# Laying out the node stages of a four-layer graph network in another order, with more turns between a tile's stages

## The reference

```python
h = relu(layernorm(x)); x = x + gcn(h)      # scatter-add over edges, W, norms, LN, relu, + h
h = relu(layernorm(x)); x = x + attn(h)     # 8-head edge attention, skip, LN, GELU FFN (512), LN
h = relu(layernorm(x)); x = x + gat(h)      # GAT with 3 heads, elu, GAT with 1 head
h = relu(layernorm(x)); x = x + sage(h)     # two SAGE layers with batch norm
```

## Time and profile before

| | us |
|---|---|
| median of 3 runs (3016.8 to 3020.15) | 3018.6 |
| the profiled execution | 3018.48 |
| its span | 3016.8 |
| node stage gcn, from its first products to the first gather of the edge pass | 571 to 657.3 |
| node stage attn, from den(0) to the first gather | 1215.8 to 1351.4 |
| node stage gat1, likewise | 1925.8 to 2047.9 |

### The profile page before, as it was taken

One profiled execution on the slowest core, in us unless ns is written; L12 is line 12 of the kernel. 1 busy time (PEld: TensorE's weight loads), 2 busy tenths in 40 slices (PEclk: granted clock), 3 DMA queues, 4 the chain that ended last, 5 costly groups with the idle time before them and its releaser, 6 DMA issues.

```text
span 3016.8 us, 36316 instructions
## 1 busy us (share of the span) xinstructions
PE 2401.5 (80%) x12365; PEld 1783.0 (59%) x12365; DVE 1385.6 (46%) x2998; ACT 927.1 (31%) x1992; POOL 1374.9 (46%) x1431
## 2 busy tenths in 40 slices
PE   6799999748888986667888786685777777499998
PEld 5566666527776775455555554355777766266666
DVE  6756655447677775434454544232222222611313
ACT  4423222223333332543444443231222222300201
POOL 3200000177777773447777773327777775300000
PEclk7577778879889897767999998685555555699999
DMA  9578854049899994106777776204555554465360
GB/s 207 154 238 298 289 198 163 1 138 277 252 264 272 258 269 122 30 20 184 248 243 238 242 236 196 74 19 102 137 129 136 130 136 106 145 202 166 118 202 27
DMA packets 518578, 517.76 MB, mean 172 GB/s; under 512 B 154113, under 2 KB 463748, under 8 KB 517212
## 3 DMA queue, kind: packets, MB, share of 16 engines
q1 hardware_dynamic: 310333, 267.24, 29.6%
q0 software_dynamic: 50528, 115.22, 15.1%
q10 hardware_dynamic: 157534, 132.98, 14.3%
HBM read 301.13 MB, written 227.33 MB: 175 GB/s over the span
## 4 chain that ended last, share of the span: by engine, by line
PE 35%; POOL 33%; issue 13%; DVE 9%; DMA 6%; ACT 4%; SPq 1%; POOLq 0%; ACTq 0%; DVEq 0%
POOL arena L1020 31%; PE ps L1529 10%; PE ps L1432 7%; PE ps L1442 7%; DMA arena<-t_gat,src_i 3%; PE ps L1511 2%; DMA arena<-t_attn,src_i 2%; ACT arena L1051 1%; PE ps L1726 1%; DVE arena L2248 1%; PE ps L1602 1%; DVE arena L1905 1%; PE ps L1703 1%; PE ps L1635 1%; PE ps L1765 1%
## 5 line engine op out<-in xcount | busy, mean ns | idle before, releaser
L1051 ACT ACTIVATE arena<-ps 128x544 f32<-128x544 f32 (+9 forms) x591 | 480.4, 823 | 1557.5 <-PE ps L1602 616.2
L1020 POOL DMA_INDIRECT arena<-t_gat,src_i x784 | 740.2, 944 | 238.9 <-issue 233.2
L1602 PE MATMUL ps<-arena 128*128 128x136 f32 (+2 forms) x2352 | 649.5, 436 | 109.9 <-ACT arena L1051 55.2
L1602 PEld LDWEIGHTS ps<-arena 128*128 128x128 f32 x2352 | 445.5, 252 | 242.9 <-DVE arena L2248 91.6
L1020 POOL DMA_INDIRECT arena<-t_attn,src_i x392 | 383.2, 978 | 119.5 <-issue 115.2
L1529 PE MATMUL ps<-arena 128*128 128x384 bf16 x1850 | 305.7, 329 | 34.4 <-DVE rec L2390 33.1
L1578 PEld LDWEIGHTS ps<-arena 128*128 128x128 f32 x1568 | 286.5, 267 | 34.9 <-issue 6.4
L2196 DVE TENSOR_TENSOR z_b<-arena,ps 128x12 f32<-128x12 f32 (+1 forms) x196 | 31.9, 163 | 565.4 <-DMA arena<-t_gat,src_i 512.1
L1529 PEld LDWEIGHTS ps<-arena 128*128 128x128 bf16 x1850 | 182.1, 99 | 157.8 <-issue 40.3
L1578 PE MATMUL ps<-arena 128*128 128x3 f32 (+1 forms) x1568 | 266.3, 292 | 5.5 <-ACT arena L1051 4.2
L1442 PE MATMUL ps<-arena 128*128 128x100 bf16 x1176 | 224.2, 364 | 27.1 <-DVE arena L2025 18.5
(11 more groups left out here) (319 smaller groups left out, 2952.2 us busy)
## 6 DMA issues: line engine op xcount, KB each, us to landing
ends_gat<-arena ACTq DMA_DIRECT2D x98, 774.0 KB
arena<-adj_hbm SPq DMA_DIRECT2D x90, 640.0 KB, 4.0
same_b<-same_hbm SPq DMA_DIRECT2D x294, 128.0 KB
adj_hbm<-arena SPq DMA_DIRECT2D x9, 3200.0 KB, 12.3
ends_attn<-arena ACTq DMA_DIRECT2D x98, 272.0 KB
ends_gat<-arena ACTq DMA_DIRECT2D x98, 258.0 KB
arena<-edst SPq DMA_DIRECT2D x98, 256.0 KB, 4.5
starts_q<-zrow SPq DMA_DIRECT2D x28, 896.0 KB, 6.6
```

The lines of the kernel that those rows point to most:

```text
L1020: g.indirect_dma_start(out=row_b[:, n % RB, k, 0:row_tab[p].shape[1]], out_offset=None, in_=row_tab[p], in_offset=bass.IndirectOffsetOnAxi ...
L1051: return a.activation(o, i, ACT.Copy)
L1602: i = mm(o, same_f[:, g % RB, k, :], msg[:, g % 4, k * W:(k + 1) * W], start=True, stop=True)
```

## The change

The lists of names and lags of the three stages are written anew; steps and waits are the same.

```diff
--- before.py
+++ after.py
@@ -478,23 +478,23 @@
         pool_o.lay("n0", ("hn", 0), ("r1", 1))
         act_o.lay("n0", ("hi", 0), ("mid", 1))
         dve_o.lay("n0", ("r2", 0))
-        pe_o.lay("gcn", ("lin", 0), ("tr", 3), ("qkv", 3))
-        act_o.lay("gcn", ("scl", 0), ("sda", 1), ("apa", 1), ("hc", 3), ("sdb", 2), ("apb", 2))
-        dve_o.lay("gcn", ("yb", 1), ("bna", 1), ("aga", 1), ("rel", 2), ("xad", 2), ("rsa", 1), ("nma", 1),
-                  ("bnb", 2), ("agb", 2), ("tab", 4), ("skp", 4), ("rsb", 2), ("nmb", 2))
-        pool_o.lay("gcn", ("ga", 1), ("ba", 1), ("bsk", 4))
-
-        pe_o.lay("attn", ("tr3", 2), ("tr2", 0), ("f0", 0), ("f1", 0), ("f2", 0), ("f3", 0), ("elr", 2), ("ffn2", 0))
-        act_o.lay("attn", ("sda", 0), ("sdc", 2), ("apa", 0), ("apc", 2), ("yc", 0), ("sdb", 1), ("apb", 1), ("hc", 2),
-                  ("g0", 0), ("g1", 0), ("g2", 0), ("g3", 0))
-        dve_o.lay("attn", ("den", 0), ("rec", 0), ("num", 0), ("y0", 0), ("bna", 0), ("aga", 0), ("xad", 2), ("bnc", 2),
-                  ("agc", 2), ("rsa", 0), ("nma", 0), ("rsc", 2), ("nmc", 2), ("el", 3), ("ga", 0), ("ba", 0),
-                  ("z", 1), ("bnb", 1), ("agb", 1), ("rsb", 1), ("nmb", 1))
-        pool_o.lay("attn", ("gb", 1), ("bb", 1))
-
-        pe_o.lay("gat1", ("tr", 0), ("feat", 2), ("lin", 0), apart=("feat",))
-        act_o.lay("gat1", ("tc", 0), ("neg", 0), ("pos", 0), ("ex", 0))
-        dve_o.lay("gat1", ("den", 0), ("rec", 0), ("num", 0), ("elu", 1), ("out", 2), apart=("out",))
+        pe_o.lay("gcn", ("tr", 3), ("lin", 0), ("qkv", 3))
+        act_o.lay("gcn", ("hc", 3), ("scl", 0), ("sda", 1), ("apa", 1), ("sdb", 2), ("apb", 2))
+        dve_o.lay("gcn", ("tab", 4), ("skp", 4), ("yb", 1), ("bna", 1), ("aga", 1), ("rel", 2), ("xad", 2),
+                  ("rsa", 1), ("nma", 1), ("bnb", 2), ("agb", 2), ("rsb", 2), ("nmb", 2))
+        pool_o.lay("gcn", ("bsk", 4), ("ga", 1), ("ba", 1))
+
+        pe_o.lay("attn", ("ffn2", 2), ("f0", 1), ("f1", 1), ("f2", 1), ("f3", 1), ("tr3", 4), ("tr2", 0), ("elr", 4))
+        act_o.lay("attn", ("sda", 0), ("sdb", 3), ("sdc", 4), ("apa", 0), ("apb", 3), ("apc", 4),
+                  ("g0", 1), ("g1", 1), ("g2", 1), ("g3", 1), ("hc", 4), ("yc", 0))
+        dve_o.lay("attn", ("el", 5), ("den", 0), ("rec", 0), ("num", 0), ("y0", 0), ("bna", 0), ("aga", 0),
+                  ("z", 3), ("bnb", 3), ("agb", 3), ("xad", 4), ("bnc", 4), ("agc", 4), ("rsa", 0), ("nma", 0),
+                  ("rsb", 3), ("nmb", 3), ("rsc", 4), ("nmc", 4), ("ga", 0), ("ba", 0))
+        pool_o.lay("attn", ("gb", 3), ("bb", 3))
+
+        pe_o.lay("gat1", ("lin", 1), ("tr", 0), ("feat", 3), apart=("feat",))
+        act_o.lay("gat1", ("neg", 1), ("pos", 1), ("ex", 1), ("tc", 0))
+        dve_o.lay("gat1", ("den", 0), ("rec", 0), ("num", 0), ("elu", 2), ("out", 3), apart=("out",))
 
         act_o.lay("gat2", ("sda", 0), ("mid", 1), ("apa", 0), ("hi", 0))
         dve_o.lay("gat2", ("den", 0), ("rec", 0), ("num", 0), ("yr", 0), ("xad", 0), ("bna", 0), ("aga", 0), ("r1", 1),
```

## The result

The changed kernel takes 3027.8 us (median of 17 runs, 3023.8 to 3038.0), the kernel before 3019.0 (17 runs beside them, 3013.1 to 3023.7). The ratio is 1.0030, 95% interval 1.0023 to 1.0038: slower by about 9 us, which is over the 0.2% bound. The profiled execution took 3033.3 us (span 3031.6), so it lies 5.5 us above its median.

The account below looks back on a forecast made before the run. The stages were taken as bound by loops of waits between engines, with no engine full. GCN -7.5, attention +2.8 and GAT 1 +11.4 sum to +6.7 us on 3018.6: 3025.2 us, range 3013 to 3035.

Parts of the forecast that it names:

- GCN -7.5: GCN stage: bsk(0) 5.7 us earlier, POOL's work 2.3 us shorter, 0.5 taken off for collisions with DVE: 7.5 us faster.
- from there POOL is the bound: GCN after bsk(0): POOL's scatters and elementwise steps set the time, 49.7 us where POOL now needs 52.0.
- The comparison of 8.4 with 9.3 us a turn: GCN: DVE's busy time of 8.4 us a turn is no tighter bound than POOL's full turn of 9.3.
- The rule on the shared port: GCN: by the skill, DVE and POOL SBUF steps lock each other out; the sum took 0.5 us, following the mean row.
- Attention +2.8: Attention stage: turns, stores and part of the lower clock's cost in ffn2, 2.8 us slower; ends -7 and +9.1.
- The loop itself: Attention after four turns: el at the head of DVE's turn waits for elr, a closed loop of 18.4 us a turn.
- "+6.2" and "+5.0": Attention: extra us if ffn2 runs at the lower clock in turns 6 and 7; somewhat under half of 11.2 was taken.
- GAT 1 +11.4: GAT 1 stage: neg(1) to neg(5) 79.7 us against 67.6, drain 19.9 against 20.6: 11.4 us slower.
- "Nothing overlaps": GAT 1: lin, tr, feat, neg, pos, ex and tc run one after another, 20.2 us a turn with lin slowed.
- (b): Rival, chance 0.10: TensorE keeps its upper clock through the new pauses of attention and GAT 1; -11 us, 3007.
- (a): Rival, chance 0.27: ffn2 slow only in turn 5, upper clock in half of GAT 1's turns; -2.2 us, 3016.
- (c): Rival, chance 0.13: the clock falls ahead of every burst and GCN's gain is half eaten on POOL; +17.6 us, 3036.

Follow-up runs that it names:

- Attention alone: Attention's lists as in the changed kernel, GCN and GAT 1 as in the kernel before: 3023.6 us, ratio 1.0008 to the kernel before.
- the filled kernel: Attention's new lists, rest as in the kernel before, plus three unread 512-wide products ahead of ffn2's wait for z: ratios 0.9988 and 0.9965 to the kernel before.
- the added products: GAT 1's new lists, rest as in the kernel before, plus five unread 512-wide products ahead of lin from turn 3 on: ratio 1.0007 to the kernel before.
- el late: Attention's new lists with el moved from the head of DVE's round to behind nmc, rest as in the kernel before: ratios 0.9965 and 0.9950 to it.
- the combined kernel: GCN's new lists, attention's with el behind nmc, GAT 1's with feat and out two rounds behind: ratios 0.9868 and 0.9872 to the kernel before.

## Why the prediction was right, step by step

The forecast was 3025.2 us with a range of 3013 to 3035; the median is 3027.8. The mechanisms were the right ones. Several sizes missed, in both directions, and that the total came so close (+6.7 forecast, +8.9 by the medians) is in part luck: attention's terms cancelled.

- **GCN -7.5, measured -6.4.** Two errors. bsk(0) came 7.5 us earlier, not 5.7: qkv(0) ran directly behind tr and lin, at the upper clock, and took 3.75 us, where the sum kept the 6.5 of the earlier trace rows, which ran at a mean granted clock of 0.55 after a pause of 2.87 us. tab did not follow at once, but 1.2 us later (596.05), behind the statistics that DVE had ahead of it. And "from there POOL is the bound" failed at the end: POOL needed 53.0 us, not 49.7. The comparison of 8.4 with 9.3 us a turn used POOL's full turn; turns 4 and 5 have little or no ga and ba left, 6.2 us of POOL, and there DVE's and TensorE's chain sets the pace. That is the 2.66 us before bsk(5), with two terms on its chain that the sum had at nothing: the transposes and qkv(5) at the lower clock (1.11 and 5.57 us for 0.66 and 3.70, so 2.3 more), and 1.1 us that rel(5) lost to POOL (next point). The scatters and elementwise steps themselves were 50.4, against 50.2 with the 0.5 for collisions.
- **The rule on the shared port.** For POOL's sum, taking the mean row was right: the full steps beside DVE's took 1.26 to 1.67 us, so at most 0.4 us was lost in one. But the sum asked only what POOL loses. DVE lost more, in steps with two inputs in SBUF that began just after one of POOL's:

```profile
600.23 0.66 DVE L2360 SCALAR_TENSOR_TENSOR arena<-arena,h_sb 128x512 f32<-128x512 f32 x1
...
608.60 1.26 POOL L997 TENSOR_TENSOR h_sb<-h_sb,r_L_gnn_bskip 128x512 f32<-128x512 f32 x1
...
608.74 1.67 DVE L2360 SCALAR_TENSOR_TENSOR arena<-arena,h_sb 128x512 f32<-128x512 f32 x1
```

  With bsk at the head of POOL's round, rel of three full turns falls on it and takes 1.66 to 1.74 us in place of 0.66; in the kernel before that of one full turn did, with 1.22. The Trainium skill ("SBUF — State Buffer", Who interferes with whom) has whoever comes second wait until the other's instruction is over, and here the trace agrees: rel ends 0.55 us after bsk does, and POOL's steps lose no more than what is left of a DVE step of 0.7 us.
- **Attention +2.8, profiled +3.8, means +1.9.** The total was right by cancelling. Turns 0 to 4: forecast 50.8, measured 54.9, since ffn2 went low already in turn 4, which had no term. (Attention alone, where it did not go low there, took 52.0.) The pause of 1.34 us ahead of it comes from the shared port as well: two steps of turn 4 met POOL's gb and bb and took 3.1 us together (1242.51 and 1244.02, 1.48 and 1.64) in place of 1.4, and z, for which ffn2 waited, stood behind them. Turn 5: 23.3, measured 21.7. Turn 6: 15.2, measured 20.2, and turn 7: 11.9, measured 14.8, both within the "+6.2" and "+5.0" left as an end, of which the sum had taken somewhat under half. The pauses ahead of these two were 2.51 and 1.02 us and not 3 to 4, and the clock fell all the same. The last turns and stores: 32.3, measured 27.8. The loop itself stood: its 18.4 us at the upper clock are what the filled kernel shows (17.7 to 19.6), and el, released by elr, was the named wait.
- **GAT 1 +11.4, measured +15.6 in the profile, +13.9 in the means.** "Nothing overlaps" held to 0.3 us: 20.45 a turn against 20.2, the rest being lin at the lower clock, 7.3 in place of 6.95. neg(1) to neg(5) took 80.8 us, forecast 79.7. The drain up to the gathers took 28.6 us, forecast 26.8: the last feats were taken as before, but one began at the lower clock (9.7 us for 36 products). The rest, 1.3 us, lies ahead of neg(1).
- **The rivals.** (b), the clock staying up through the pauses, did not come: every lin of GAT 1 began low and four ffn2 ran low. (a), half of the turns at the upper clock, is out for GAT 1: no lin of a full turn after a pause of 3.8 us or more began at the upper one, in any trace. Its support was thin from the start. The feat of 2.88 us in the earlier trace rows is the best of four that followed a pause of 3.37 us in the kernel before; the other three took 5.53, 4.17 and 4.45 us, all or in part at the lower clock:

```profile
1960.20 5.53 PE L1765 MATMUL ps<-w,arena 128*128 128x258 f32 x12 [3.37 <-DVE h_sb L2440]
```

  A level that changes from turn to turn has to be read over all turns, not from one row. (c) was right in its mechanism, the clock falling ahead of nearly every burst, and wrong in its other half, since only 1 of GCN's 7.5 us was lost. By the rule behind it (the Trainium skill, "TensorE: Matmul & The Clock Gate", HAM oscillation — how this bites in real kernels) each burst of a waiting loop starts throttled: in GAT 1 the trace agrees, with 2.1 us per turn, which the added products gave back; in attention it agrees for the ffn2 after 4.24 and 2.51 us, while the two after 1.34 and 1.02 us began at the upper level and fell while they ran.

What the forecast did not ask is how near a better order lay. The sum named neg's wait for feat(i-3) as what closes the loop, and never priced feat(i-2).

## What to carry to other kernels

A hand-written order is judged by its loops: for each engine take the step at the head of its round and follow what it waits for. If that was issued last in another engine's round, the round is a barrier, however many turns lie between; moving that one step took 39 us off GAT 1 (feat one lag closer), and 7 to 8.5 us off attention beyond what the clock takes (el behind nmc), with the same steps in each. Two engines that share a port are a term of their own: a step moved to the head of a round can fall on the other engine's, and the loss shows on the engine that came second. Where a loop leaves TensorE standing, add the clock's price to the loop's, and when a steady bound is computed, check it again for the last turns, where the steps that fill the bounding engine have run out.

## What the runs showed of the hardware

TensorE's lower level (granted 0.50, 1.2 GHz) came in the changed kernel's attention stage after pauses as short as 1.34 and 1.02 us, some 2 and 1 us into ffn2's 128-wide products and not at their start, and lasted to the end of that ffn2; the clock came back only within the products of f behind it. The same pause did not always do it: in five other traces with the same steps up to that point (attention alone, and el late and the combined kernel twice each) ffn2 of turn 4 stayed at the upper level after 1.33 to 1.35 us. From the first run of el late:

```profile
1517.56 0.45 PE L1724 MATMUL ps<-r_L_gnn_bf,ones 1*128 1x128 f32 x2 [1.35 <-DVE arena L2343]
...
1522.44 1.16 PE L1726 MATMUL ps<-w_f,arena 128*128 128x128 f32 x8
```

So the length of the last pause alone did not tell which level followed. Three 512-wide products in the pause of turn 5 (4.24 us without them) kept ffn2 at the upper level over the 1.48 us that were left: 5.9 us in both filled traces, 10.7 in both without.

In all eight traces of chips 3 and 8 TensorE stood for some 6 us early in the attention stage with nothing that the profile shows to wait for; in the six of the other chips it did not. Nor is that a matter of this stage: in the first edge pass (690 to 1200 us) 86 to 114 us of TensorE's idle time stand under "issue" in each of the eight traces, and 1.1 us in each of the six.

VectorE (DVE) and GpSimd (POOL) held each other up in elementwise steps that read SBUF: a DVE step of 0.66 us with two inputs in SBUF took 1.67 us when it began 0.14 us after one of POOL's, and one of POOL's of 1.26 us took up to 1.67 beside DVE's.
